# One attention and expert kernel: light steps of both halves first, and normalisation on ScalarE

## The reference

```python
h = layernorm(du, ln1_w, ln1_b)
q, k, v = split(h @ in_proj_w.T + in_proj_b)
attn = softmax(causal(q . k / 4)) . v          # over positions t <= s, per row b
x1 = du + attn @ out_proj_w.T + out_proj_b
h2 = layernorm(x1, ln2_w, ln2_b)
gates = top 2 of softmax(h2 @ router_w.T) over 8 experts
y = sum over experts of (gelu(h2 @ w1[e]) * gate) @ w2[e]      # w1 256x512, w2 512x256
out = x + x1 + y
```

## Time and profile before

| | us |
|---|---|
| median of 3 runs | 748.74 (745.62 to 749.02) |
| the profiled execution | 748.15 |
| its span, first to last instruction | 746.4 |
| TensorE busy | 611.9 (82%) |
| VectorE busy | 436.1 (58%) |
| ScalarE busy | 353.0 (47%) |
| POOL busy | 456.7 (61%) |
| last x1 written (L857) | 554.50 |

### The profile page before, as it was taken

The page is one execution under the profiler, slowest core; times in us unless marked ns, Lnnn a source line. Parts: engine busy times, 40 slices in busy tenths (PEclk is TensorE's granted clock), DMA queues, the critical chain, the costliest instruction groups (busy, mean ns, idle before and its releaser), DMA issues. The chain is left out here.

```text
span 746.4 us, 10164 instructions
## 1 busy us (share of the span) xinstructions
PE 611.9 (82%) x2640; PEld 405.9 (54%) x2640; DVE 436.1 (58%) x1028; ACT 353.0 (47%) x817; POOL 456.7 (61%) x560
## 2 busy tenths in 40 slices
PE   2668897657657579879789999999699999999992
PEld 1334454335434446546556656667476676767671
DVE  1266899999599953646876589979944000011110
ACT  4343343131232236756666665656357555544440
POOL 6777676488744743687768866583375844444342
PEclk9998888587688789979979999999989999999997
DMA  4366653112311122243222433253244543444432
GB/s 122 120 223 193 206 154 105 44 58 80 87 43 38 33 60 44 58 111 70 50 57 52 87 57 50 39 97 56 36 87 80 123 75 66 65 72 67 65 54 26
DMA packets 51547, 59.83 MB, mean 80 GB/s; under 512 B 7386, under 2 KB 47075, under 8 KB 51428
## 3 DMA queue, kind: packets, MB, share of 16 engines
q0 software_dynamic: 18288, 23.28, 19.3%
q1 hardware_dynamic: 33204, 35.91, 16.7%
HBM read 35.89 MB, written 27.46 MB: 85 GB/s over the span
## 5 line engine op out<-in xcount | busy, mean ns | idle before, releaser
L433 POOL DMA_INDIRECT out_dram<-y,xin x71 | 117.4, 1653 | 42.9 <-issue 33.6
L966 PE MATMUL b_y<-w_s,hm_hmT 128*128 x568 | 135.0, 381 | 6.6 <-ACT y L535 5.8
L951 PE MATMUL b_h<-w_s,xT 128*128 x284 | 136.1, 602 | 1.6 <-ACT xT L496 1.6
L966 PEld LDWEIGHTS b_y<-w_s,hm_hmT 128*128 128x128 f32 x568 | 102.4, 190 | 20.0 <-issue 9.0
L1087 PE MATMUL b_at<-ident,pv_prod 128*128 128x128 f32 x544 | 79.2, 298 | 30.7 <-DVE pv_prod L897 30.7
L668 DVE TENSOR_SCALAR y<-b_y,xin,live 128x256 f32<-128x256 f32 x24 | 13.1, 544 | 141.8 <-PE b_y L966 141.8
L831 DVE TENSOR_TENSOR qk_prod<-q,kv 128x1024 f32<-128x1024 f32 (+2 forms) x80 | 88.1, 1125 | 5.0 <-ACT kv L565 4.2
L897 DVE TENSOR_TENSOR pv_prod<-kv,pr 128x1024 f32<-128x1024 f32 (+2 forms) x80 | 84.0, 1095 | 11.4 <-PE b_at L1087 11.3
L1087 PEld LDWEIGHTS b_at<-ident,pv_prod 128*128 128x128 f32 x544 | 70.6, 159 | 33.8 <-issue 32.5
L1043 PE MATMUL b_qk<-wqkv,hT 128*128 128x512 f32 x128 | 85.3, 802 | 0.0
L839 DVE TENSOR_REDUCE sc<-qk_prod 128x64 f32<-128x1024 f32 (+2 forms) x80 | 82.2, 1052 | 0.3
(11 more groups left out here) (166 smaller groups left out, 1045.7 us busy)
## 6 DMA issues: line engine op xcount, KB each, us to landing
xin<-xs_d SPq DMA_DIRECT2D x71, 132.5 KB, 2.1
w_s<-in_L_ffn_w_dram SPq DMA_DIRECT2D x16, 512.0 KB, 4.6
xp<-in_x_dram SPq DMA_DIRECT2D x32, 128.0 KB
xud<-in_x_dram SPq DMA_DIRECT2D x32, 128.0 KB
out_dram<-x POOLq DMA_DIRECT2D x32, 128.0 KB, 3.3
xud<-in_x_dram SPq DMA_DIRECT2D x32, 126.0 KB
out_dram<-y,xin POOLq DMA_INDIRECT x71
xud<-in_x_dram SPq DMA_DIRECT2D x64, 1.0 KB
```

What stands on the lines that cost most here:

```text
L433: pool.indirect_dma_start(out_rows, bass.IndirectOffsetOnAxis(ap=xin[:, j % NX, H:H + 1].bitcast(U32), axis=0), y[:, j % NY, :], None, com ...
L951: mm = pe.matmul(b_h[:, :], xT[:, k * P:(k + 1) * P], w1_s[:, bass.ds(e * (HC * F) + k * F, F)], start=(k == 0), stop=(k == HC - 1))
L966: mm = pe.matmul(b_y[:, 0:H], hmT[:, k * P:(k + 1) * P], w2_s[:, bass.ds(e * (FC * H) + k * H, H)], start=(k == 0), stop=(k == FC - 1))
```

## The change

The order of steps becomes a list, `ORDER`: positions 0 to 3 of the first half of the rows, positions 0 to 3 of the second half, then positions 4 to 15 of the first and 4 to 15 of the second. Keys and values of positions 0 to 3 of the second half get slots of their own (`kv` grows from 32 to 40 slots of 256), and the wait at the reuse of slots moves from step 16 to step 20 (`AGAIN`). `zrow`, the row of zeros of the prefix DMAs, becomes a part of the last `xin` buffer, so SP waits for these DMAs before it loads tile 5 in place of the last group's first tile. `WANT` is rewritten. With it tile 0 is prepared in iteration 13 as before, tiles 0 to 7 stand in iterations 16 to 19 (two each), 8 in 20, 9 in 21, 10 to 15 in 22 to 24, none in 25, 16 to 27 in 26 to 31 (two each), 28 to 30 in 32 to 34, and 40 come behind the loop.

`unit` moves from VectorE to ScalarE, where it stands first in the iteration. It computes x * rstd + shift in one activation. POOL makes shift = -mean * rstd by one tensor_scalar more behind each rstd, linked to it by a semaphore.

```diff
@@ -30,6 +30,10 @@
     E, _, F = w1.shape
     HC, FC = H // P, F // P
     G = B // P * S
+    FEW = 4
+    ORDER = [(c, p) for a, b in ((0, FEW), (FEW, S)) for c in range(B // P) for p in range(a, b)]
+    AGAIN = S + FEW
+    KV = S + FEW
     ENDS = (5, 9, 13, 18, 23, 27, G)
     GROUPS = [range(a, b) for a, b in zip((0,) + ENDS, ENDS)]
     NG = len(GROUPS)
...
@@ -89,7 +92,7 @@
         w1_s = sb("w1_s", [P, E * HC * F])
         w2_s = sb("w2_s", [P, E * FC * H])
 
-        kv = sb("kv", [P, 2 * S, H])
+        kv = sb("kv", [P, 2 * KV, H])
         xp = sb("xp", [P, 2, H + 2])
         xud = sb("xud", [P, 2, 2, H])
         du = sb("du", [P, DU, H])
...
@@ -165,7 +170,7 @@
         blo = pv_prod[0:1, 0, :].bitcast(F32R)
 
 
-        NPIECE = [(g % S) // TP + 1 for g in range(G)]
+        NPIECE = [p // TP + 1 for c, p in ORDER]
         PIECES = [sum(NPIECE[:g]) for g in range(G + 1)]
 
 
@@ -186,7 +191,7 @@
         PLACES = {0: (), 1: (0,), 2: (0, 1), 3: (0, 1, 2), 4: (0, 0, 1, 2)}
         LATER = {1: (2,), 2: (3, 4), 3: (2, 3, 4)}
 
-        WANT = [0] * 10 + [1, 1, 1, 2, 2, 2, 2] + [2, 1, 1, 1, 1, 1, 2, 2] + [2, 2, 2, 2, 2, 2, 2] + [1, 1, 1]
+        WANT = [0] * 13 + [2] * 7 + [1] * 2 + [2] * 10 + [1] * 3
 
         def group_of(j):
             return [r for r in range(NG) if j >= FIRST[r]][-1]
...
@@ -207,7 +212,7 @@
 
         def projected_late(g):
 
-            return g > S
+            return g > AGAIN
 
         W1_FROM = 1
         W2_FROM = 3
@@ -230,7 +235,16 @@
             return y_added[j % 2], 16 * (j // 2 + 1)
 
         def half_of(g):
-            return g // S, g % S
+            return ORDER[g]
+
+        def keys_at(g, t):
+
+            c, _ = ORDER[g]
+            return S + t if c and t < FEW else t
+
+        def values_at(g, t):
+
+            return KV + keys_at(g, t)
 
         block = ctx.enter_context(nc.Block())
 
@@ -287,8 +301,8 @@
                     r = group_of(j)
                     sp.wait_ge(s["tab_ready"], r + 1)
                     sp.wait_ge(scattered[r], 32 * len(GROUPS[r]))
-                    if r == NG - 1:
-                        sp.wait_ge(s["pre_done"], 16 * E)
+                if j == NX - 1:
+                    sp.wait_ge(s["pre_done"], 16 * E)
                 if j >= NX:
                     sp.wait_ge(*added_to(j - NX))
                 row = sp.value_load(tabr[0:1, j:j + 1], min_val=0, max_val=E * CAP - P)
...
@@ -390,7 +404,9 @@
                 pool.wait_ge(s[("stats1", "stats2")[k]], g + 1)
                 i = g % 2
                 link(pool.tensor_scalar(rstd[:, k, i:i + 1], mv[:, k, i, 1:2], EPS, None, ALU.add))
-                pool.tensor_tensor(rstd[:, k, i:i + 1], rstd[:, k, i:i + 1], power[:, :], ALU.pow).then_inc(s[("rstd1", "rstd2")[k]], 1)
+                link(pool.tensor_tensor(rstd[:, k, i:i + 1], rstd[:, k, i:i + 1], power[:, :], ALU.pow))
+                pool.tensor_scalar(shift[:, k, i:i + 1], mv[:, k, i, 0:1], rstd[:, k, i:i + 1], -1.0, ALU.mult,
+                                   ALU.mult).then_inc(s[("rstd1", "rstd2")[k]], 1)
 
             def scatter(g):
 
...
@@ -552,22 +568,22 @@
                     slot(j)
 
             def exponentials(g):
-                n = NH * (g % S + 1)
+                n = NH * (half_of(g)[1] + 1)
                 act.wait_ge(s["sc_ready"], g + 1)
                 act.activation(pr[:, g % 2, 0:n], sc[:, g % 2, 0:n], ACT.Exp, scale=SCALE).then_inc(s["exp_ready"], 1)
 
             def queries_keys(g):
-                p = g % S
+                p = half_of(g)[1]
                 act.wait_ge(s["qkv_ready"], g + 1)
                 act.activation(q[:, g % 2, :], b_qk[:, 0:H], ACT.Copy).then_inc(s["qk_sb"], 1)
-                if p == 0 and g > 0:
+                if g == AGAIN:
                     act.wait_ge(s["sc_ready"], g)
-                act.activation(kv[:, p, :], b_qk[:, H:2 * H], ACT.Copy).then_inc(s["qk_sb"], 1)
+                act.activation(kv[:, keys_at(g, p), :], b_qk[:, H:2 * H], ACT.Copy).then_inc(s["qk_sb"], 1)
 
             def values(g):
-                if g == S:
-                    act.wait_ge(s["pv_piece"], PIECES[S - 1] + 1)
-                act.activation(kv[:, S + g % S, :], b_v[:, 0:H], ACT.Copy).then_inc(s["v_sb"], 1)
+                if g == AGAIN:
+                    act.wait_ge(s["pv_piece"], PIECES[AGAIN - 1] + FEW // TP + 1)
+                act.activation(kv[:, values_at(g, half_of(g)[1]), :], b_v[:, 0:H], ACT.Copy).then_inc(s["v_sb"], 1)
 
             def odds(r):
 
@@ -577,7 +593,23 @@
 
             act.wait_ge(s["alpha_ready"], 1)
             act.activation(junk[:, 1:2], alpha[:, 0, 0:1], ACT.Copy)
+            def unit(src, g, k):
+
+                act.wait_ge(s[("rstd1", "rstd2")[k]], g + 1)
+                if k == 0 and g >= 2:
+                    act.wait_ge(s["hT_ready"], g - 1)
+                if k == 1 and g >= RING:
+                    r = [r for r in range(NG) if g - RING in GROUPS[r]][0]
+                    act.wait_ge(scattered[r], 32 * len(GROUPS[r]))
+                dst = hn[:, g % 2, :] if k == 0 else ring[:, g % RING, 0:H]
+                act.activation(dst, src, ACT.Identity, scale=rstd[:, k, g % 2:g % 2 + 1],
+                               bias=shift[:, k, g % 2:g % 2 + 1]).then_inc(s[("xhat1", "xhat2")[k]], 1)
+
             for g in range(-AHEAD, G + 3):
+                if 0 <= g - 3 < G:
+                    unit(x1[:, (g - 3) % 4, :], g - 3, 1)
+                if 0 <= g + 2 < G:
+                    unit(du[:, (g + 2) % DU, :], g + 2, 0)
                 if 0 <= g - 2 < G:
                     act.wait_ge(s["pv_used"], PIECES[g - 1])
                     if g - 2 >= 1:
@@ -597,11 +629,11 @@
                     odds(ROUTE[g - 1])
                 if g >= 0 and SLOTS[g, 0] and g < G:
                     act.activation(junk[:, 0:1], junk[:, 1:2], ACT.Gelu)
-                if g == S:
-                    values(S)
+                if g == AGAIN:
+                    values(g)
                 if 0 <= g + 1 < G:
                     queries_keys(g + 1)
-                    if g + 1 != S:
+                    if g + 1 != AGAIN:
                         values(g + 1)
                 place(g, 0)
                 if 0 <= g + 2 < G:
...
@@ -813,10 +833,6 @@
                         dve.wait_ge(s["xhat1"], g + 2)
                     dve.bn_aggr(mv[:, 0, (g + 3) % 2, :], small[:, 48:54]).then_inc(s["stats1"], 1)
 
-                if 0 <= g - 3 < G:
-                    unit(x1[:, (g - 3) % 4, :], g - 3, 1)
-                if 0 <= g + 2 < G:
-                    unit(du[:, (g + 2) % DU, :], g + 2, 0)
                 if 0 <= g < G:
                     scv = sc[:, g % 2, 0:NH * T].rearrange("p (n t) -> p n t", t=T)
                     dve.wait_ge(s["qk_sb"], 2 * (g + 1))
@@ -831,7 +847,7 @@
                         made.append(tick(dve.tensor_tensor(
                             qk_prod[:, m % 2, 0:(t1 - t0) * H].rearrange("p (t h) -> p t h", h=H),
                             q[:, g % 2, :].rearrange("p (o h) -> p o h", o=1).to_broadcast([P, t1 - t0, H]),
-                            kv[:, t0:t1, :], ALU.mult)))
+                            kv[:, keys_at(g, t0):keys_at(g, t0) + t1 - t0, :], ALU.mult)))
 
                     def add_up(m):
                         t0, t1 = m * TP, min(T, m * TP + TP)
...
```

More of the change, by code:

```diff
@@ L113, in adaln_moe_block @@
         rstd = sb("rstd", [P, 2, 2])
+        shift = sb("shift", [P, 2, 2])
         power = sb("power", [P, 1])
@@ L134, in adaln_moe_block @@
         xin = sb("xin", [P, NX, ROW])
+        zrow = xin[:, NX - 1, :]
         y = sb("y", [P, NY, H])
@@ L200, in adaln_moe_block @@
         for g in range(G + 3):
-            for n in (PLACES if g != S else LATER)[WANT[g]]:
+            for n in (PLACES if g != AGAIN else LATER)[WANT[g]]:
                 if scattered_by(group_of(max(at + 3, 0))) < g:
@@ L361, in later_constants @@
                             pool.iota(iota_i[:, TMAX + 3 * E:TMAX + 3 * E + 1], [[1, 1]], base=0, channel_multiplier=1),
-                            pool.iota(idt[:, :].rearrange("p (c s) -> p c s", c=G // S), [[P, G // S], [B, S]], base=0,
-                                      channel_multiplier=1)]
+                            *[pool.iota(idt[:, g:g + n], [[B, n]], base=p * B + c * P, channel_multiplier=1)
+                              for g, c, p, n in ((0, 0, 0, FEW), (FEW, 1, 0, FEW), (2 * FEW, 0, FEW, S - FEW), (AGAIN, 1, FEW, S - FEW))]]
                 links_of.append(pool.iota(iota_w[:, :].rearrange("p (a b) -> p a b", b=2), [[16, ALL // 2 + 1], [0, 2]],
@@ L366, in later_constants @@
                 link(links_of[-1])
-                link(pool.memset(zrow[:, :], 0.0))
+                link(pool.memset(zrow, 0.0))
                 pool.tensor_copy(iota_f[:, :], iota_i[:, :])
@@ L479, in scale @@
             def scale(g):
-                i, p = g % 2, g % S
+                i, (_, p) = g % 2, half_of(g)
                 if g == 0:
@@ L648, in _ @@
```

(12 more changed lines are left out.)

9 lines of the change are left out of this document (4 added, 5 removed).

## The result

The changed kernel is slower: 765.58 us (median of 4 runs, 761.81 to 769.32) against 748.88 (4 runs, 745.62 to 750.39), a ratio of 1.023 with a 95% interval of 1.017 to 1.029, so the loss itself is clear of the noise, and whether it reaches 2% is not. Forecast were 723 us, with a range of 702 to 745. The profiled execution took 765.47 us, its span 763.7.

What follows compares the result with a forecast made beforehand. No engine bounds the whole: a TensorE-ScalarE ring in light intervals, VectorE in heavy ones, TensorE and VectorE nearly both later. Stretches summed to 533.3 us at the last x1, plus 189.55 of tail: 723 us, range 702 to 745.

Steps and rivals of the forecast that it cites:

- Start: Up to x1 of step 0: POOL's extra operation per rstd adds 2.0 us to 49.41, giving 51.4.
- Light intervals 3 to 9: Few keys, no tiles: two activations between logits and aT add 1.0 us to 10.27 each; seven take 79 us.
- Intervals 10 to 13: Row prices 16, 11.4, 12.2 and 13, plus 10 for a stall behind POOL's scatters and prefix DMAs: 62.6 us.
- Heavy intervals 14 to 19: Many keys: 122.73 us less the 8.62 stall and 6.6 for units leaving VectorE, 107.5 us.
- the eight tiles "at nothing": Tiles in iterations 16 to 19: no added time, hidden in TensorE's idle time while VectorE bounds.
- The turn, 20 and 21, and 22: Turn to the second half, 20 and 21: 42 us (40 to 46); interval 22 with one tile: 12.9 us.
- 23 to 33: 191.23 us less 2.7 in 23, 4.2 in 26, 3 in 28 to 31 and 3.5 in 32: 177.8 us.
- Tail: Behind the last x1: 193.65 us with one tile fewer, 189.55; tail tiles stay at 4.10 each.
- the third rival: Late rstd from POOL holds ScalarE's queue and TensorE, 2 us in each of intervals 15 to 33: 761 us; chance 0.08.
- The first: ScalarE becomes the serial bound, units ahead of aT: +1.2 in 14 filled intervals, 17 more, 740 us; chance 0.18.
- The second: Heavy steps don't cover their tiles: 4 us in each of intervals 17 to 20, 16 more, 739 us; chance 0.10.
- The fourth: Light ring isn't lengthened and the prefix is hidden: 19 us less, 704 us; chance 0.12.

Runs made afterwards that it cites:

- e3_fill: Changed kernel plus fillers: TensorE turns the identity twenty times in each of iterations 3 to 12, result unused; 744.23 us.
- e8_order_fill: Kernel before with the new order and tile lists, units on VectorE, plus unused TensorE turns of the identity in iterations 3 to 12; 731.15 us.
- e6_apart: Changed kernel with the second tile of iterations 16 to 19 moved behind the first piece of value products on TensorE; 757.47 us.
- e1_order: Kernel before with only the new order of steps and tile lists; both units stay on VectorE, no shift on POOL; 737.60 us.
- e4_uncovered: Changed kernel without the eight tiles of iterations 16 to 19, tile 0 left in iteration 13; 25 tiles in the loop, 46 behind it; 780.80 us.
- e12_no24: Changed kernel without the two tiles of iteration 24; 29 tiles in the loop and 42 behind it; 766.70 us.

## Why the prediction was wrong, step by step

The sum was 723; the profiled run is 42.6 above it (765.47 against 722.85 before rounding). Interval by interval:

- **Start.** 51.4 foreseen, 51.68 measured. Right.
- **Light intervals 3 to 9.** 79.1 foreseen, 92.4 measured: 13.3, the largest miss. That the units lengthen a ring was right. The failed step is its size: +1.0 an interval, with +2.0 (12.3) as the upper bound where the clock doesn't stay high or the units don't fit in a gap. Measured was +3.4 in intervals 4 to 8 (13.7). At an unchanged clock +1.0 was about right: the units cost 0.63 at 1.00 (e3_fill against e8_order_fill) and 0.9 at 0.83 (e6_apart against e1_order). What failed is that the clock was taken to stay at 0.83, and it fell to 0.62. The 0.83 of the earlier trace rows was the mean of intervals that swung, 3 and 4 for instance:

```profile
49.41:58.22 8.81, 6.60 (x24) 3.58 (x24) 6.84 (x16) 4.01 (x12) 6.94 (x12) 0.95 0.81 283
58.22:69.65 11.43, 9.73 (x30) 5.30 (x30) 7.32 (x18) 4.20 (x13) 6.55 (x12) 0.74 0.55 152
```

  I read it as a state of the stage, not as a thing that the change could push. A bound could have been worked out from rows of before: TensorE's 34.48 us for four intervals at 0.83, wholly at 1.2 GHz, are by this estimate about 34.48 x 0.83 / 0.5 = 57 us, 14.3 an interval with no wait at all. By that the end was above 14, not 12.3.
- **Intervals 10 to 13.** 62.6 foreseen, 65.9 measured. The stall came where it was put, for the reason given; interval 13 took 25.32 where 13 + 10 were foreseen. It was seen as a wait of 12.60 us of TensorE for the ring, behind ScalarE's waits for POOL (10.45 for xud, 1.70 for shift). The rest of the miss is interval 12, 15.33 where 12.2 were foreseen, with 10 and 11 shorter than foreseen (15.12 and 10.14); why it is long was not traced.
- **Heavy intervals 14 to 19.** 107.5 foreseen, 117.9 measured. The relief of VectorE was rightly sized: it was busy 101.4 us in them against 108.5 in e1_order, 7.1 less, where I had 6.6. But it is worth 2.2 in 14 to 16, and in 17 to 19, where tiles stand, the changed kernel is 2.8 slower than e1_order. The failed step is the eight tiles "at nothing": they cost 16.0 us in 17 to 20 (e4_uncovered). I took the sum of idle time as cover. The intervals 28 to 31 that I leaned on were themselves 95% full on TensorE, which shows that both engines can be full, not that a tile adds nothing to the interval that it joins.
- **The turn, 20 and 21, and 22.** 42 foreseen, 44.6 measured; 12.9 and 12.8. The first holds part of the same tiles' price.
- **23 to 33.** 177.8 foreseen, 185.8 measured, 6.4 of it in interval 26: 19.86 instead of 13.5, though it has no tiles. ScalarE in order of time there:

```profile
443.41 0.60 ACT L503 ACTIVATE du<-xp,alpha 128x256 f32<-128x256 f32 x1 [4.02 <-DMA xud<-in_x_dram]
446.67 0.51 ACT L506 ACTIVATE xud<-xud,z 128x256 f32<-128x256 f32 x1 [2.66 <-POOL xud L391]
...
449.94 0.60 ACT L605 ACTIVATE ring<-x,shift,rstd 128x256 f32<-128x256 f32 x1 [2.30 <-POOL shift L408]
```

  It waits 9.0 us, first for x itself and then for POOL. e1_order has 18.78 there, so most of it is the order's. My step took VectorE as the bound because no tile stood there, and left out four scatters and the adds of the tiles before. How the wait divides between POOL and the late load of x stays open: e12_no24 moved 2.2 us of it, and no kernel moved the load.
- **Tail.** 189.55 foreseen, 194.43 measured. e1_order has 738.30 - 547.79 = 190.5, so the order's part was right; the rest is a wait that I had not looked for, behind the last steps. The chain of waits of the changed kernel (start, us, what):

```profile
577.08 0.97 POOL xs_d L417
...
578.45 0.58 POOL rstd L407
...
579.12 0.28 POOL shift L408
...
579.42 0.61 ACT ring L605
580.03 0.04 issue
580.08 0.69 PE b_tr L1070 x2
```

  TensorE waited 4.63 us for that turn with tiles queued behind it. Here POOL came late, as the third rival had it.

**The rivals.** The first (ScalarE the serial bound) named the right place, the units ahead of aT, and the wrong price. It put 17 us on 14 filled intervals, where the units cost 6.4 (17 to 33, against e1_order); the damage was in the seven light ones, by way of the clock, where no chance was given to anything over 12.3. The second (cover) came out at its price: 16 us foreseen, 16.0 measured. Both together make 756; the range ended at 745. The third (POOL late in 19 intervals) did not carry: ScalarE waited 25.0 us for ring's shift in the whole run, in 10 iterations, where 38 were priced. The fourth, that the ring isn't lengthened, is out.

The Trainium skill spoke of it in two places. Its page "ScalarE: Activation LUTs" (Rules for kernel authors) keeps add and mul on VectorE; the unit took 0.60 us there against 0.51 by its formula, which is for one pointer operand where the unit has two. Its advice came out right here, but for the place in the queue and the clock, not for the price of an element. Its page "TensorE: Matmul & The Clock Gate" (A second HAM failure mode) says that short idle times between groups of matmuls can make the clock swing, which e3_fill bears out. Its remark in Part 1 that the ramp costs under 1% of a typical kernel is on the first warming up, which no run here has apart, and is no bound for a clock that falls again: the fillers bring back 21.3 of 765.6 us, 2.8%.
